# Edge phase of a two-layer graph network: types by transfers, a third PSUM buffer, later sums and another order of stages

## The reference

```python
m = x[src] * rel[edge_type]
m = jnp.concatenate([m[:half] @ W_in, m[half:] @ W_out], 0)
deg = jax.ops.segment_sum(jnp.ones((e,), x.dtype), dst, num_segments=n)
norm = 1.0 / jnp.maximum(deg, 1.0)
agg = jax.ops.segment_sum(m * norm[dst][:, None], dst, num_segments=n)
return jnp.tanh(agg + x @ W_loop + b)
```

## Time and profile before

| what | value |
|---|---|
| median of 3 runs | 2799.92 us (2799.6 to 2803.63) |
| span of the profiled execution | 3183.3 us |
| time of the profiled execution over the median | 383.4 us |
| TensorE busy | 2759.1 us (87%) |
| VectorE busy | 2303.9 us (72%) |
| GpSimd busy | 1952.0 us (61%) |
| ScalarE busy | 1865.5 us (59%) |

### The profile page before, as it was taken

The page is one execution under the profiler, slowest core; times in us unless marked ns, Lnnn a source line. Parts: engine busy times, 40 slices in busy tenths (PEclk is TensorE's granted clock), DMA queues, the critical chain, the costliest instruction groups (busy, mean ns, idle before and its releaser), DMA issues. The chain is left out here.

```text
span 3183.3 us, 55393 instructions
## 1 busy us (share of the span) xinstructions
PE 2759.1 (87%) x20688; PEld 2587.3 (81%) x20688; DVE 2303.9 (72%) x3258; ACT 1865.5 (59%) x3179; POOL 1952.0 (61%) x2129
## 2 busy tenths in 40 slices
PE   4888888888888888797888888888888887997998
PEld 3888888888888888796877887878777786997998
DVE  6777777777677777896777777777777776995665
ACT  6556665555555555585555555555555554785444
POOL 6666666666666666455666666666666664892223
PEclk9999989999999999899999999999999999998999
DMA  8333333333333333353333333333333333452221
GB/s 259 119 90 89 89 89 90 89 89 90 88 89 90 90 88 90 92 164 104 90 90 90 89 90 92 88 90 90 89 89 92 88 90 98 136 158 90 69 67 64
DMA packets 162458, 312.57 MB, mean 98 GB/s; under 512 B 34061, under 2 KB 95309, under 8 KB 162229
## 3 DMA queue, kind: packets, MB, share of 16 engines
q0 software_dynamic: 79872, 218.21, 23.8%
q1 hardware_dynamic: 81120, 89.89, 8.8%
q10 hardware_dynamic: 1237, 1.41, 0.2%
HBM read 263.90 MB, written 45.48 MB: 97 GB/s over the span
## 5 line engine op out<-in xcount | busy, mean ns | idle before, releaser
L740 PE MATMUL edge_rg<-edge_rel_hi,edge_hot 128*128 128x256 f32 x6656 | 1551.7, 293 | 86.6 <-issue 63.0
L740 PE MATMUL edge_rg<-edge_rel_lo,edge_hot 128*128 128x256 f32 x4992 | 1312.3, 289 | 60.0 <-issue 58.9
L740 PEld LDWEIGHTS edge_rg<-edge_rel_hi,edge_hot 128*128 128x128 f32 x6656 | 1219.6, 197 | 143.7 <-issue 92.2
L548 ACT ACTIVATE edge_hot<-edge_typ,minus_type 128x512 fp32r<-128x512 f32 x832 | 526.8, 685 | 935.9 <-DMA dense_prev<-emb_t 383.9
L740 PEld LDWEIGHTS edge_rg<-edge_rel_lo,edge_hot 128*128 128x128 f32 x4992 | 983.1, 197 | 70.0 <-issue 68.5
L623 DVE TENSOR_TENSOR edge_m_lo<-edge_rg,edge_m_hi 128x1024 fp32r<-128x1024 f32 x416 | 509.3, 1224 | 241.3 <-ACT edge_m_hi L541 127.7
L604 DVE TENSOR_SCALAR edge_hot<-edge_typ,type_of 128x512 fp32r<-128x512 f32 x832 | 582.3, 741 | 12.4 <-ACT edge_hot L548 8.7
L753 PE MATMUL edge_small<-edge_m_hi,edge_sel 128*128 128x258 f32 x1664 | 458.1, 306 | 96.3 <-DVE edge_m_lo L623 90.7
L530 POOL DMA_INDIRECT edge_xg<-emb,src x416 | 399.0, 959 | 225.9 <-issue 96.2
L530 POOL DMA_INDIRECT work<-h,src x416 | 400.7, 963 | 221.9 <-issue 101.9
L530 POOL DMA_INDIRECT edge_xg<-h,src x416 | 400.2, 962 | 216.2 <-issue 102.8
(11 more groups left out here) (183 smaller groups left out, 3933.9 us busy)
## 6 DMA issues: line engine op xcount, KB each, us to landing
work<-emb,src POOLq DMA_INDIRECT x416
edge_xg<-emb,src POOLq DMA_INDIRECT x416
work<-h,src POOLq DMA_INDIRECT x416
edge_xg<-h,src POOLq DMA_INDIRECT x416
set_x_rows<-in_x SPq DMA_DIRECT2D x25, 256.0 KB, 3.9
emb<-set_e_rows SPq DMA_DIRECT2D x25, 256.0 KB, 2.9
emb_t<-acc SPq DMA_DIRECT2D x5, 1280.0 KB
dense_prev<-emb_t SPq DMA_DIRECT2D x25, 256.0 KB, 2.7
```

The lines of the kernel that those rows point to most:

```text
L548: act.activation(hot[:, q % 2, c], typ[q % 2][:], ACT.Abs, bias=K["minus_type"][:, c:c + 1]).then_inc(distances, 1)
L740: ins = pe.matmul(rg[q % 2][:, t, :], hot[:, q % 2, c, t * P:(t + 1) * P], part[:, c, :], start=(c == 0 and part is rel_hi), stop=(c == FULL))
```

## The change

- The setup converts the types to int16 and stores them in DRAM. SyncE loads them back for each pair of groups, broadcast over all 128 partitions (load_types), and the matmul that spread them, its PSUM tiles and the table ident_r go.
- The freed PSUM gives rg a third buffer. VectorE's message and low part and ScalarE's high part move from lag 2 to lag 3.
- The sums move a turn later: TensorE's one_window and turn_over from lag 4 to SUMS_LAG = 5, VectorE's add_window likewise, ScalarE's copy_sums from lag 3 to 5.
- ScalarE's list begins with high; VectorE's one-hots stand between message and the low part.
- distance and VectorE's one_hot now wait for rel_done of the group two before (the one whose one-hot buffer they overwrite); before, the matmul of the types stood behind those matmuls on TensorE.

```diff
@@ phase_setup @@
-            act.copy(K["typ"][0:TYPE_ROWS], types_i[0:TYPE_ROWS]).then_inc(tables, 1)
+            act.copy(types_s[0:TYPE_ROWS], types_i[0:TYPE_ROWS]).then_inc(types_short, 1)
+            act.wait_ge(types_short, 1)
+            act.dma_start(types_out, types_s[0:TYPE_ROWS]).then_inc(types_stored, 16)
...
@@ phase_edges: buffers and SyncE @@
+        typ = s.sb("typ", [P, 2, 2 * GROUP * P], I16)
-        rg = [s.ps(f"rg{b}", [P, GROUP, DIM]) for b in range(2)]
-        typ = [s.ps(f"typ{b}", [P, GROUP * P]) for b in range(2)]
+        rg = [s.ps(f"rg{b}", [P, GROUP, DIM]) for b in range(RG_RING)]
...
+            def load_types(p):
+
+                wait_past(sp, hot_done, 2 * p - 2)
+                wait_past(sp, distances, HOT_ACT * (2 * p - 2))
+                sp.dma_start(typ[:, p % 2], types[p:p + 1, :].rearrange("o k -> (o k)").partition_broadcast(P))\
+                  .then_inc(typ_in[p % 2], 16)
+
+            load_types(0)
+            load_types(1)
             sp.dma_start(rel_sb[:, 0:FULL, :], rel[0:FULL * P, :].rearrange("(c p) d -> p c d", p=P))\
               .then_inc(rel_in, 16)
...
@@ phase_edges: GpSimd's gathers @@
+                wait_past(pool, messages, g - GROUPS_IN_RING + 1)
@@ phase_edges: ScalarE @@
                     act.wait_ge(messages, g + 1)
+                    if bank is by_three:
+                        wait_past(act, windowed, g - 1)
...
             def distance(g, q, i):
 
 
-                act.wait_ge(typ_done, g + 1)
+                act.wait_ge(typ_in[q // 2], 16 * (i + 1))
+                wait_past(act, rel_done, g - 1)
...
                 if q % 2 == 1:
-                    act.wait_ge(summed, g // 2 + 1)
+                    act.wait_ge(windowed, g + 1)
                     act.copy(sums_sb[:, q // 2], sums[q // 2][0:WIN, :]).then_inc(sums_copied, 1)
...
-                over_groups(act, (0, later(distance)), (2, high), (0, later(one_hot)), (3, copy_sums), (0, clear_one))
+                over_groups(act, (3, high(by_three)), (0, later(distance)), (0, later(one_hot)),
+                            (SUMS_LAG, copy_sums), (0, clear_one))
@@ phase_edges: VectorE @@
-                dve.wait_ge(distances, HOT_ACT * (g + 1))
-
+                dve.wait_ge(typ_in[q // 2], 16 * (i + 1))
+                wait_past(dve, rel_done, g - 1)
                 for c in range(HOT_ACT, RCHUNKS):
-                    ins = dve.tensor_scalar(hot[:, q % 2, c], typ[q % 2][:], K["type_of"][:, c:c + 1], None,
+                    ins = dve.tensor_scalar(hot[:, q % 2, c], types_of(q), K["type_of"][:, c:c + 1], None,
                                             ALU.is_equal)
...
-                over_groups(dve, (2, message), (2, one_window), (4, add_window), (2, low), (0, one_hot_later))
+                over_groups(dve, (3, message(by_three)), (0, one_hot_later), (3, one_window), (SUMS_LAG, add_window),
+                            (3, low(by_three)))
@@ phase_edges: TensorE @@
-                pe.matmul(typ[q % 2][:], row, K["typ"][0:TYPE_ROWS, q % 2 * GROUP * P:(q % 2 + 1) * GROUP * P],
-                          start=True, stop=True).then_inc(typ_done, 1)
...
-                over_groups(pe, (4, one_window), (2, relation_rows), (0, spread_later), (4, turn_over))
+                over_groups(pe, (SUMS_LAG, one_window), (2, relation_rows(by_three)), (SUMS_LAG, turn_over))
```

More of the change, by code:

```diff
@@ L47 @@
 HOT_ACT = 2
+RG_RING = 3
+SUMS_LAG = 5
 CLEAR_AT = 32
@@ L427, in over_groups, with phase_edges @@
         turn(STEPS + t // GROUPS_IN_RING, t % GROUPS_IN_RING)
-def phase_edges(nc, K, layer, nodes, rel, nodes_t, matrices):
+def phase_edges(nc, K, layer, types, nodes, rel, nodes_t, matrices):
     first = layer == 0
@@ L457, in phase_edges, with types_of, by_three, by_two @@
         sums_t = [v[:, 512 - (DC + 1) * WIN:].rearrange("p (k n) -> p k n", n=WIN) for v in small]
+        def types_of(q):
+            return typ[:, q // 2, q % 2 * GROUP * P:(q % 2 + 1) * GROUP * P]
+        def by_three(g, q):
+            return g % RG_RING
+        def by_two(g, q):
+            return q % 2
         def sel_at(q, t, width):
@@ L465, in phase_edges @@
         rel_split = s.sem("rel_split")
-        picked = s.sem("picked")
-        typ_done = s.sem("typ_done")
+        typ_in = [s.sem(f"typ_in{b}") for b in range(2)]
         gathered = [s.sem(f"gathered{q}") for q in range(GROUPS_IN_RING)]
@@ L505, in _ @@
                                  columns(K, chunks).rearrange("p c k n -> p c (k n)")).then_inc(columns_out, 16)
+            for p in range(2, PAIRS):
+                load_types(p)
             sp.wait_ge(messages, GROUPS - 2)
@@ L590, in _ @@
                         clear(c)
-                over_groups(act, (0, later(distance)), (2, high), (0, later(one_hot)), rolled=True)
+                over_groups(act, (0, later(distance)), (2, high(by_two)), (0, later(one_hot)), rolled=True)
             with act.Else():
-                over_groups(act, (0, later(distance)), (2, high), (0, later(one_hot)), (3, copy_sums), (0, clear_one))
+                over_groups(act, (3, high(by_three)), (0, later(distance)), (0, later(one_hot)),
+                            (SUMS_LAG, copy_sums), (0, clear_one))
         @block.vector
@@ L610, in one_hot_later, with message, stage, low @@
                     one_hot(g, q, i)
[L612 to L624, removed]
+            def message(bank):
+                def stage(g, q, i):
+                    at = slice(GROUP * (q % 2), GROUP * (q % 2 + 1))
+                    rows = rg[bank(g, q)]
+                    dve.wait_ge(gathered[q], 16 * GROUP * (i + 1))
+                    dve.wait_ge(rel_done, g + 1)
+                    dve.tensor_tensor(rows[:], xg[q // 2][:, at, :], rows[:], ALU.mult).then_inc(messages, 1)
+                return stage
+            def low(bank):
+                def stage(g, q, i):
+                    dve.wait_ge(hi_done, g + 1)
+                    dve.tensor_tensor(m_lo[:, q % 2], rg[bank(g, q)][:], m_hi[:, q % 2, :, 0:DIM].bitcast(F32),
+                                      ALU.subtract).then_inc(lo_done, 1)
+                return stage
             def select(out, dst):
@@ L689, in all_windows @@
                         add(0, w * WIN, half_at + w * WIN).then_inc(win_added, 1)
-                over_groups(dve, (0, pick_row), (2, message), (2, low), (0, one_hot_later), (3, all_windows),
+                over_groups(dve, (2, message(by_two)), (0, one_hot_later), (2, low(by_two)), (3, all_windows),
                             rolled=True)
@@ L726, in spread_later, with relation_rows, stage @@
[L726 to L744, removed]
+            def relation_rows(bank):
+                def stage(g, q, i):
+                    if isinstance(g, int) and g == 0:
+                        pe.wait_ge(rel_split, 3)
+                        pe.wait_ge(filled, 3)
+                    pe.wait_ge(hot_done, g + 1)
+                    pe.wait_ge(hot_act, g + 1)
+                    rows = rg[bank(g, q)]
+                    for t in range(GROUP):
+                        for c in range(RCHUNKS):
+                            for part in (rel_hi, rel_lo) if c < FULL else (rel_hi,):
+                                ins = pe.matmul(rows[:, t, :], hot[:, q % 2, c, t * P:(t + 1) * P], part[:, c, :],
+                                                start=(c == 0 and part is rel_hi), stop=(c == FULL))
+                        if t < GROUP - 1:
+                            ins.then_inc(rel_tile, 1)
+                    ins.then_inc(rel_done, 1)
+                return stage
@@ L1579, in build @@
 def build(nc, a, out):
+    types = nc.dram_tensor("types", [TYPE_ROWS, 2 * GROUP * P], I16, kind="Internal").ap()
     emb = nc.dram_tensor("emb", [NODES_PAD, DIM], F32, kind="Internal").ap()
```

51 lines of the change are left out of this document (20 added, 31 removed).

## The result

The changed kernel takes 3534.5 us (median of 4 runs, 3534.3 to 3535.8), the old one 2800.4 beside it: 1.262 times as long (95% interval 1.260 to 1.264). Forecast were 3498, between 3080 and 3590.

A forecast was written before the change was run, and what follows sets the result against it. Gathers (5.0 us a group) and TensorE (4.89) were both taken as close bounds. Forecast: 690.6 outside the edge phases + 2793 for TensorE's cycles with stalls and clock falls + 2 × (4 + 3) = 3498 us, range 3080 to 3590.

The forecast's parts named there:

- The stall: TensorE waits before its transposes every second turn for ScalarE's copy of the sums: 2.85 us each, 208 times.
- the cast: ScalarE's cast of the high part, ahead of distance, may still run when relation rows end: 0 to 1.0 us.
- TensorE's own work: TensorE's windows, relation matmuls and transposes over two turns, without the types' matmul: 9.28 us a cycle.
- the 12.13 without clock falls: TensorE's cycle of two turns, own work plus stall at full clock: 12.13 us, 6.07 a group.
- The clock: TensorE's granted clock falls around the stalls, 1.5 us a fall: 1.3 us a cycle, bounds 0 and 1.7.
- 14 of 16: Share of TensorE's long edge-phase waits with a clock fall in or just behind them, applied to the new stalls.
- Types, loads, third buffer at nothing: Hidden loads, one-hots from SBUF, third buffer: 0 each; TensorE's saved types' matmul was already left out of 12.13.
- One sign named: Expected in the profile after: GpSimd idle longer, its gathers still 0.95 us each.
- gathers beside the one-hots: GpSimd's gathers slowed by VectorE's one-hots from SBUF: 5.0 up to 6.0 us a group, hidden under 6.07.
- The old kernel: Plain runs of the old kernel: 5.07 us a group in the edge phases, 690.6 us outside them.
- The rival of a stall without clock falls: TensorE stalls before its transposes but keeps its clock: 3228 us, chance 0.20.
- The faster rival: ScalarE copies the sums before TensorE needs them, no stall, gathers' floor 5.0 to 5.03 a group: 2785 us, chance 0.04.

The follow-up runs named there:

- e4: Changed kernel with 20 unread matmuls on TensorE between relation rows and transposes of every second turn; 3244.6 us, ratio 1.156.
- e5: e1 without the loads of types after the first two pairs; 2878.2 us.
- e9: Changed kernel with VectorE's two one-hots reading the relation buffer in PSUM and waiting for ScalarE's cast of it; 3670.7 us.
- e1: Changed kernel with ScalarE's copy of the sums moved ahead of distance and one_hot; 2880.0 us, ratio 1.027 to the old kernel.
- e7: Types by transfers alone: two relation buffers, old lags and old lists on ScalarE and VectorE; 2905.0 us, ratio 1.038.
- e0: The old kernel run again unchanged, for a profile that is not late; 2802.0 us.
- e2: Changed kernel with the transposes and additions one turn later (lag 6), the copy left in place; 2892.9 us, ratio 1.031.
- e8: e1 with VectorE's two one-hots reading the relation buffer in PSUM, after a wait for ScalarE's cast of it; 3036.1 us.
- e10: e7 with VectorE's two one-hots reading the relation buffer in PSUM, with no wait added; 2812.0 us, ratio 1.004 to the old kernel.
- e3: Old kernel with ScalarE's copy of the sums at lag 4 in place of 3; 3900.8 us, ratio 1.390.

## Why the prediction was right

- *The stall.* Right in place, number and releaser: 208, before L795, released by L599, 626 us. Taken were 2.85 us a stall from the last matmul's step; the timeline above has 1811.77 to 1815.00, 3.2. Of the missing 0.4 some 0.3 is the cast, the term with bounds of 0 and 1.0 that the sum all but left out: it ended at 1812.42, and the distances began at 1812.32, where VectorE's one-hots, which wait for the same matmuls, began at 1812.04. The distances' 1.24, near the upper of their bounds, are the other 0.1.
- *TensorE's own work.* Taken as 9.28 a cycle, from rows with a gap at the start of each block. In the changed kernel those gaps are nearly gone: 12.12 (the cycle of e4) less 3.2 leaves 8.9. This and the stall's 0.4 cancel, so that the 12.13 without clock falls was met by luck, by two errors of opposite sign.
- *The clock.* Predicted 1.3 a cycle from 1.5 for 14 of 16. 198 of 206 cycles had a fall, and the medians of the two cycles differ by 13.57 − 12.12 = 1.45, close to the 1.5. Over all cycles the two runs differ by 3534.5 − 3244.6 = 290 us, 1.39 for each of 208. The term was small by 0.1 a cycle, some 20 us of the 36 by which the time was off. The other 17 are the 3244.6 of e4 against the 3228 predicted without falls; as the median cycle was met, they lie at the ends of the phases and outside them (693.9 against 690.6). Here the rule of the Trainium skill ("TensorE: Matmul & The Clock Gate", "HAM oscillation — how this bites in real kernels"), that such a loop pays in every pass, came nearer than the share of 14 in 16; the trace agrees with it in 198 of 206 cycles. That the falls come from TensorE's idle time in the stall is shown by e4, where the stall is as long and filled and no cycle has one.
- *Types, loads, third buffer at nothing.* Right for the loads (e5, without the stall). For the one-hots from SBUF it fits that the stall hid them: GpSimd idles 294 us before one quarter of its gathers in the changed kernel, so it is not the pace-maker there. The run that was to show it, e9, is inconclusive. Without the stall the longer gathers cost the 75 to 100 us of e1 and e7. One sign named was wrong: the gathers did not stay at 0.95, their mean in the changed kernel is 0.99, as the prediction's own part on gathers beside the one-hots has it. The bound given, 6.0 us a group, was far above the 5.18 to 5.27 measured.
- *The old kernel.* The 5.07 a group and the 690.6 outside were worked out from one late profile and held in e0 (5.07 and 691.9). The prediction left it open whether gathers (5.0) or TensorE (4.89) pace it; e0 shows the gathers.
- The rival of a stall without clock falls, 3228, is what e4 ran: 3244.6. The faster rival's condition (the copy done before TensorE needs it) is e1 and e2; it came to 2880 and 2893, not 2785, since the longer gathers set a pace of 5.18 to 5.25 us a group in place of 5.0.

## What to carry to other kernels

When stages of one turn are shifted on several in-order engines, look for the shortest loop that a shift closes: here the copy moved by two turns and its reader by one. Before, TensorE had a turn of relation rows to do between the two; now it waits for five ScalarE instructions, and the first four can start only after its last relation matmul. Where the copy stands within ScalarE's list decided 655 us. In these runs work taken from TensorE, which was not the pace-maker, gained nothing, and moving a VectorE source from PSUM to SBUF slowed the gathers that were.

## What was unexpected of the hardware

A gather that starts beside one of VectorE's one-hots with all sources in SBUF often takes 1.15 to 1.2 us in place of 0.95: of the gathers in e7 that started beside a one-hot from SBUF 81% took over 1.05 us, in e1 58%, and beside the destinations' one-hot 65% and all of 124. Beside message and low part, which have one source in PSUM, and one-hots from PSUM it was 0 to 2% in e1, e7, e8 and e10. The Trainium skill ("SBUF — State Buffer", "Who interferes with whom") has VectorE and GpSimd share a pair of SBUF ports, which a VectorE instruction takes in a two-port mode, or in part with two sources in SBUF, where it gets in the way of GpSimd instructions that read SBUF. The runs agree as far as the destinations' one-hot has two sources in SBUF, and message and low part have one; whether the types' one-hot ran in such a mode, and what a gather reads, no run here shows. The gather's loss here, 0.2 us, is less than the 0.48 that the one-hot lasts.

In e3 the slower clock lasted longer behind a stall of 3.8 us than it did in the changed kernel behind one of 3.1 (20 slow steps a cycle against 15). The cause stays open.
